# Attention of layer 1: the near values of a head searched in three parts instead of four

## The reference

```
KEEP = int(1024 * 0.3)                     # 307
qkv = layernorm(x) @ W_qkv.T + b_qkv       # 16 heads of 8
scores = q @ k.T * 128 ** -0.5             # 1024 x 1024 for each head
keep the 307 largest of each row, softmax over them, times v
```

## Time and profile before

| | us |
|---|---|
| median of 3 runs | 3681.74 |
| lowest, highest | 3681.28, 3684.51 |
| profiled execution | 3686.02 |
| its span, first to last instruction | 3684.3 |

### The profile page before, as it was taken

How to read it: one execution, slowest core, us unless ns; L and a number is a source line. 1 busy time by engine, 2 the same in 40 slices (tenths; PEclk the granted TensorE clock), 3 DMA queues, 4 the chain that set the end, 5 groups by cost and what they waited for, 6 DMA issues and landing times. The chain is left out here.

```text
span 3684.3 us, 83752 instructions
## 1 busy us (share of the span) xinstructions
PE 2778.2 (75%) x24345; PEld 1606.7 (44%) x24345; DVE 2745.3 (75%) x9136; ACT 2498.8 (68%) x4058; POOL 1953.7 (53%) x4541
## 2 busy tenths in 40 slices
PE   3399999667745777777777777776777777757999
PEld 2033333233423545444444544444454445445665
DVE  6677777235448988888888888887889888844444
ACT  2066666533128999989999989997889989832222
POOL 3023333410228777777777777776777777730000
PEclk9599999888656776777777766776666776777999
DMA  3111111000230101101100100110100110010000
GB/s 111 53 51 51 47 48 41 14 26 20 71 53 2 15 4 17 17 3 17 17 6 13 17 12 8 17 16 3 17 8 12 17 14 5 2 31 3 6 6 9
DMA packets 114079, 82.54 MB, mean 22 GB/s; under 512 B 57897, under 2 KB 97083, under 8 KB 113595
## 3 DMA queue, kind: packets, MB, share of 16 engines
q1 hardware_dynamic: 105403, 72.18, 9.1%
q0 software_dynamic: 8192, 4.79, 0.9%
HBM read 54.25 MB, written 19.40 MB: 20 GB/s over the span
## 5 line engine op out<-in xcount | busy, mean ns | idle before, releaser
L1125 PE MATMUL a_ST<-a_qs,a_ks 75*128 75x128 bf16 x4096 | 763.7, 275 | 302.8 <-ACT a_eT L1164 289.4
L1229 POOL TENSOR_TENSOR a_near<-a_side,a_z 128x1024 int32<-128x1024 int32 x512 | 968.6, 1892 | 43.8 <-POOL a_side L1225 2.1
L1327 DVE MAX8 a_cand<-a_near 128x8 f32<-128x256 f32 x2048 | 777.0, 405 | 3.3 <-POOL a_near L1229 2.5
L1125 PEld LDWEIGHTS a_ST<-a_qs,a_ks 75*128 75x128 bf16 x4096 | 510.9, 127 | 505.9 <-issue 454.6
L1366 DVE TENSOR_SCALAR_CACHE_REDUCE a_z<-a_S,a_thr 128x1024 f32<-128x1024 f32 x512 | 645.0, 1260 | 103.5 <-issue 81.5
L1149 ACT ACTIVATE a_signs<-a_z,a_tiny 128x1024 bf16<-128x1024 f32 x512 | 587.5, 1147 | 168.0 <-DVE a_z L1366 167.1
L1142 ACT ACTIVATE a_signs<-a_S,search 128x1024 bf16<-128x1024 f32 x512 | 569.3, 1112 | 35.8 <-PE a_S L1078 35.7
L1164 ACT ACTIVATE a_eT<-a_ST 128x1024 f32<-128x1024 f32 x512 | 518.7, 1013 | 69.5 <-PE a_ST L1126 68.7
L1078 PE MATMUL a_S<-a_ks,a_qs 72*128 72x512 bf16 x1024 | 442.4, 526 | 123.4 <-DVE a_z L1366 85.4
L717 ACT ACTIVATE a_eT<-a_ST 128x512 f32<-128x512 f32 (+3 forms) x768 | 354.3, 489 | 258.7 <-PE a_ST L687 198.9
L824 DVE TENSOR_REDUCE a_mx<-a_S 128x1 f32<-128x512 f32 (+3 forms) x768 | 380.8, 547 | 114.3 <-PE a_S L674 77.2
(11 more groups left out here) (340 smaller groups left out, 4617.1 us busy)
## 6 DMA issues: line engine op xcount, KB each, us to landing
a_qs<-q_parts SPq DMA_DIRECT2D x176, 64.0 KB
a_ks<-k_parts SPq DMA_DIRECT2D x176, 64.0 KB
a_qs<-a_flip SPq DMA_DIRECT2D x512, 0.8 KB
q_parts<-p_qp SPq DMA_DIRECT2D x48, 128.0 KB, 1.7
k_parts<-p_kp SPq DMA_DIRECT2D x48, 128.0 KB, 1.8
a_qs<-q_parts SPq DMA_DIRECT2D x64, 96.0 KB
a_ks<-k_parts SPq DMA_DIRECT2D x64, 96.0 KB
f_w<-L_ffn_W SPq DMA_DIRECT2D x16, 256.0 KB, 2.8
```

The source lines that it names most:

```text
L1125: pe.matmul(ST[:, block_of], ks[:, base(hl) + kb * P:base(hl) + (kb + 1) * P], qs[:, tile(hl):tile(hl) + P], start=True, stop=False)
L1229: pool.tensor_tensor(near[:, hl % 2, :].bitcast(I32), side[:, one].bitcast(I32).broadcast_to([P, SEQ]), z[:, hl % H, :].bitcast(I32), ALU. ...
L1327: mm = dve.max(found[:, 8 * g:8 * g + 8], near[:, h2 % 2, g * SW:(g + 1) * SW])
```

## The change

The row of 1024 near values is cut at 344 and 684 instead of at 256, 512 and 768. There are 24 candidates instead of 32, one search instruction less for each tile, and `signals` has one column less (VIEWS is 21 instead of 22). The order of the searches in the three kinds of slots is adjusted:

```diff
-    SEGS, WINDOW = 4, 16
-    SW = SEQ // SEGS
+    SEGS, WINDOW = 3, 16
+    SEG_AT = (0, 344, 684, SEQ)
...
                 def top(g):
                     if has2 is not None:
-                        mm = dve.max(found[:, 8 * g:8 * g + 8], near[:, h2 % 2, g * SW:(g + 1) * SW])
+                        mm = dve.max(found[:, 8 * g:8 * g + 8], near[:, h2 % 2, SEG_AT[g]:SEG_AT[g + 1]])
...
                     top(2)
-                    top(3)
                 elif h % 2:
...
                     top(2)
-                    top(3)
                 else:
...
                     top(1)
-                    top(2)
                     if closes(it, h):
                         group = groups(it, h)
                         dve.wait_ge(flag_p, group + 1)
                         dve.tensor_scalar(seen[:, :], FL, 1.0, None, ALU.mult, ALU.add, accum_out=flag_sum[:, :]).then_inc(flag_v, 1)
-                    top(3)
+                    top(2)
```

## The result

The changed kernel takes 3846.86 us (median of 4 runs, 3845.06 to 3852.65) against 3683.12 us before (4 runs, 3681.28 to 3684.99). The ratio is 1.0447, 95% interval 1.0429 to 1.0465: 164 us slower. Forecast were 3865, from 3815 to 3905. The span of the profiled execution is 3843.4 us, 159.1 more than before.

A forecast was written before the change was run, and what follows sets the result against it. No engine was full; a chain through VectorE, ScalarE, GpSimd and TensorE was taken to bound the kernel. -11 + 3 x 23.5 + 124 = +183 us on the median of 3681.7 gave 3865 us, range 3815 to 3905.

The forecast's parts named there:

- The step that decided: Layer 1's attention: counted on the inputs, three parts overfill three rows, in tiles 99, 194 and 225; four parts overfill none.
- the short way: Repair of a flagged tile whose wanted value is still found among the candidates: 23.5 us for one tile flagged.
- the selection: Slow repair in tile 225, whose wanted value is missing from the candidates: 38 rounds over 1024 elements, 124 us, ends 105 and 158.
- the one rule: In the count of rows: the slow repair runs when the wanted value is missing from a full part's candidates; one such tile.
- The loop's own step: Loop cost per round of the slow repair, not shown in the trace: taken as 0.5 us, between 0 and 1.4.
- The ordinary path: Work of unflagged tiles, with three searches instead of four and shorter sorts: 11 us faster, ends 0 and 46.
- The pitch: Time per VectorE search back to back, 0.323 us each for 256 elements: one search fewer saves 62 ns a tile.
- only one VectorE slot of four is in it: VectorE's share in the bounding chain of a half period: two slots in eight count, so the saving is 11.4 us.
- the covered half: VectorE slots whose searches were said to run beside ScalarE and GpSimd, so that shortening them gains nothing.
- the old group: The one flagged group already in the trace before: not from an overfilled part but two equal values; the change leaves it.
- The rivals without fallbacks: No row is overfilled on the chip and the search alone counts: 3671 us, down to 3636; chance 0.05.
- without selection: Rival: tile 225's row isn't overfilled or its value is found, so only cheap fallbacks run: 3741 us; chance 0.10.

The follow-up runs named there:

- run 2: The changed kernel with its three parts cut at 388 and 704 instead of 344 and 684: 3693.34 us, ratio 1.0021 to the kernel before.
- Run 1: The changed kernel with the signal of a part compared with a never exceeded constant, so no row falls back for an overfilled part: 3666.25 us, ratio 0.9950.
- run 7: The changed kernel with two parts of 512 and 16 candidates instead of three parts: 6450.82 us, ratio 1.7509 to the kernel before.
- runs 4: The changed kernel without the call of the 38-round selection, so one row keeps a wrong set: 3728.60 us, ratio 1.0117 to the kernel before.
- Runs 9: The kernel before with three parts only in slots h % 8 = 1, 3, 4 and 5, sorts over 32, no part signals: 3677.42 us, ratio 0.9985.
- run 10: The kernel before with three parts only in slots h % 8 = 0, 2, 6 and 7, all signals kept: 3682.56 us, ratio 0.9992.
- run 11: The kernel before with three parts in all slots, sorts still over 32 candidate places, no part signals: 3675.47 us, ratio 0.9977.
- run 12: The kernel before with four searches of 256, sorts over the first 24 candidates only, no part signals: 3795.75 us, ratio 1.0300.
- run 3: The changed kernel with a narrow fourth part of 16 values cut off the last one, four searches again: 3884.86 us, ratio 1.0542 to the kernel before.
- run 6: The kernel before, four parts, with the third search moved behind L1448 in the slot where the flag is read: 3679.90 us, ratio 0.9989.
- runs 6, 8: The second of these: three parts cut at 388 and 704, second search moved behind L1448 in the flag slot: 3687.27 us, ratio 1.0009.

## Why the prediction was right

**The fallbacks.** The step that decided held in every part. Three rows were counted, and the trace has three new flagged groups with the flag at those three tiles. (They come at 1521, 1940 and 2095 us, 15 to 17 before the times that were reckoned from a mean slot.) Two went the short way, and the third ran the selection. 23.5 us were said for each; 22.1 and 23.9 are measured (26.64 and 28.50 less 4.58), and 24 in run 2; the one with the selection comes to 137.6 - 115.7 = 21.9. Run 1 shows that nothing else makes the kernel slower, run 2 that the places decide and not the width, and run 7 that the count holds for 31 tiles, with the one rule mended after its result was known.

**The selection** was priced at 124, and is 116 (runs 4 and the trace). The rounds are (2218.2 - 2109.9) / 37 = 2.93 us and not 3.14. The MAX8 of 1024 takes 1.23 (1.19 forecast), the replace 1.21 as forecast. The loop's own step, the term without a row, takes 0.26 (0.34 of idle less the 0.08 between dependent steps) instead of 0.5, so it was 9 us too dear, and the MAX8 1.5 too cheap.

**The ordinary path** was the term that was off: -11 forecast, -23 in the changed kernel's trace. The other three kernels with the same searches and sorts give 2096.8 (run 1), 2103.1 (run 2) and 2098.0 (run 4) of ordinary time, so 20, 13 and 18; the mean of the four is 19. It lies between the ends of 0 and 46. The pitch was right: 30.3 fewer busy us stand in the search row, 59 ns a tile for 62, and 12.8 in the rows of the three sorts (90.5, 88.4 and 89.5 before, 86.1, 84.2 and 85.3 after), so 43 of the 46 us of VectorE's time are seen to be saved. What failed is the step "only one VectorE slot of four is in it". Runs 9 and 10 tell against it: 5.5 us from the covered half, 3 from the other; run 11 has 8.5 from both and run 12 3.6 from the sorts. The ordinary times of their four traces agree: 5.7, 3.4, 7.8 and 3.9 under before. A part of what I missed is the longer search over the flag's load (run 3). The rest isn't settled. 8.5 + 3.6 = 12 is less than the 19 of run 1, but their intervals (3.3 us to either side for run 11, 5 for run 12, 6 for run 1) overlap, and 3.3 us of run 11's ordinary time are two of the long small instructions of run 2. In runs 6, 8 and 10 the slots behind the shortened ones are longer, so that gains don't add up slot by slot; which wait takes them isn't shown.

**The sum.** -23.5 + 22.1 + 23.9 + 137.6 (the third slot, selection in it) - 1.2 for the old group, whose stall became shorter, is +158.9, and the spans differ by 159.1 (the medians by 164). Forecast were +183: 12 of the difference are the ordinary path, 8 the selection, the rest the short ways and the old group. All four were off to the same side, so no error was hidden by another. The rivals without fallbacks (3671) and without selection (3741) are the times of runs 1 (3666) and 4 (3729) within 12 us; so these were the right other cases, and the three rows decided between them.

No version that keeps every repair is clearly faster than the kernel before: run 6 gains 4 us and run 10 3 us, with intervals that begin at about 1 and at 0. Runs 1, 9 and 11 gain more, but leave the repair of overfilled rows out.

## What to carry to other kernels

A fast path with an exact but slow fallback has two prices, and only one of them stands in the profile. Before the fast path is made narrower, count on the data how often the fallback will run, and read its price from the one time that it occurs; here 3 rows of 65,536 cost 184 us, nearly eight times the 23 us saved over all 512 tiles. Where a chain of engines turns in a fixed order, don't credit an edit with the slots in which it looks bound: measure halves of it, since a shorter slot can be given back two slots later.

## What the runs showed of the hardware

The time of VectorE's search goes with its length over the whole span measured: means of 151 ns at 16 elements, 405 at 256, 502 at 344, 677 at 512 and 1228 at 1024, which is 1.04 to 1.10 ns an element between neighbours (run 3, the changed kernel, run 7, the selection). The 1.02 that I had taken from 32 and 256 elements was a little low (256 to 1024 give 1.07), which is where the 1.19 for 1024 comes from. A loop on the engine costs 0.34 us of idle from the end of one round's last instruction to the next round's first, where no register is read from memory, against 1.2 to 1.7 us a pass with a flag read and a branch. An instruction of 0.16 us on VectorE can take 1.85 at the start of a pass of a long loop (run 2).
